# Two expert layers of a decoder on one core: sums copied out by token half, normalization shared between VectorE and ScalarE, last rows stored in two pieces

## What is computed

```python
def _layernorm(x, axis=-1, eps=1e-05):
    m = jnp.mean(x, axis=axis, keepdims=True)
    v = jnp.var(x, axis=axis, keepdims=True)
    return (x - m) / jnp.sqrt(v + eps)

x = _layernorm(x + _L0_attn_ref(x, ...))              # layer A
x = _layernorm(x + _L0_xattn_ref(x, ctx_2048, ...))   # layer B
x = _layernorm(x + _L0_ffn_ref(x, ...))               # layer C: 64 experts of 96 units, top 8
x = _layernorm(x + _L1_attn_ref(x, ...))              # layer D: linear attention
x = _layernorm(x + _L1_xattn_ref(x, ctx_2048, ...))   # layer E
x = _layernorm(x + _L1_ffn_ref(x, ...))               # layer F: 8 experts of 176 units, top 2, and a shared one of 704
```

## Time and profile before

| what | value |
|---|---|
| median of 3 runs | 999.08 us |
| lowest and highest run | 995.08 and 999.41 us |
| the profiled execution's own time | 999.09 us |
| its span, first to last instruction | 997.3 us |
| TensorE busy | 953.6 us, 96% |
| VectorE busy | 635.7 us, 64% |
| ScalarE busy | 443.1 us, 44% |
| mean granted TensorE clock | 0.991 of full |

### The profile page before, as it was taken

The page is one execution under the profiler, slowest core; times in us unless marked ns, Lnnn a source line. Parts: engine busy times, 40 slices in busy tenths (PEclk is TensorE's granted clock), DMA queues, the critical chain, the costliest instruction groups (busy, mean ns, idle before and its releaser), DMA issues. The chain is left out here.

```text
span 997.3 us, 18763 instructions
## 1 busy us (share of the span) xinstructions
PE 953.6 (96%) x6147; PEld 754.6 (76%) x6147; DVE 635.7 (64%) x1474; ACT 443.1 (44%) x862; POOL 311.9 (31%) x514
## 2 busy tenths in 40 slices
PE   6999999999999999999999999988999998999994
PEld 5788887688888888888887855667877775888883
DVE  3676777655655555555556666688778845555555
ACT  4777886432233322222222223326767773333321
POOL 1133123244444444444446303210000015344430
PEclk9999999999999999999999999999999998999997
DMA  8000000256433333333333000011111111655501
GB/s 280 23 17 18 2 2 1 57 156 185 144 133 120 112 113 109 112 111 112 112 111 103 21 0 11 6 36 36 31 37 33 32 66 25 134 145 111 112 19 42
DMA packets 37423, 75.55 MB, mean 76 GB/s; under 512 B 7121, under 2 KB 18365, under 8 KB 37222
## 3 DMA queue, kind: packets, MB, share of 16 engines
q1 hardware_dynamic: 37074, 74.53, 26.3%
q0 software_dynamic: 288, 0.23, 0.2%
HBM read 67.57 MB, written 2.40 MB: 70 GB/s over the span
## 5 line engine op out<-in xcount | busy, mean ns | idle before, releaser
L1059 PE MATMUL ps<-shared 128*128 128x512 f32 x1560 | 380.1, 393 | 0.6 <-POOL shared L2112 0.5
L1059 PEld LDWEIGHTS ps<-shared 128*128 128x128 f32 x1560 | 293.9, 189 | 66.7 <-issue 5.0
L1483 ACT ACTIVATE shared<-pT 128x512 fp32r<-128x512 f32 x130 | 82.2, 632 | 286.5 <-DVE pT L1910 286.5
L2110 POOL CAST shared<-wraw 128x512 fp32r<-128x512 f32 (+1 forms) x130 | 91.3, 703 | 298.0 <-PE ps L1085 275.4
L1913 DVE TENSOR_TENSOR al<-pT,shared 128x512 fp32r<-128x512 f32 x130 | 120.4, 926 | 92.4 <-ACT shared L1483 92.4
L1902 DVE TENSOR_TENSOR e<-e,ps 128x512 f32<-128x512 f32 x130 | 89.4, 688 | 124.4 <-PE ps L1059 120.2
L1085 PE MATMUL ps<-shared 128*128 128x512 f32 x520 | 162.0, 393 | 0.3 <-DVE al L1913 0.2
L2112 POOL TENSOR_TENSOR shared<-wraw,shared 128x512 fp32r<-128x512 f32 (+1 forms) x130 | 133.5, 1027 | 10.4
L1085 PEld LDWEIGHTS ps<-shared 128*128 128x128 f32 x520 | 97.5, 188 | 22.4 <-DVE al L1913 1.2
L1477 ACT ACTIVATE e<-ps 128x512 f32<-128x512 f32 x130 | 77.7, 598 | 77.3 <-PE ps L1059 77.3
L1910 DVE TENSOR_TENSOR pT<-e,kbd 128x512 f32<-128x512 f32 x130 | 100.0, 769 | 7.1
(11 more groups left out here) (228 smaller groups left out, 1376.7 us busy)
## 6 DMA issues: line engine op xcount, KB each, us to landing
kbd<-combine_C SPq DMA_DIRECT2D x46, 512.0 KB
wraw<-in_C_w SPq DMA_DIRECT2D x48, 384.0 KB, 8.2
kbd<-combine_F SPq DMA_DIRECT2D x15, 512.0 KB
wraw<-in_F_w SPq DMA_DIRECT2D x17, 384.0 KB, 7.0
kbd<-kbd SPq DMA_DIRECT2D x96, 32.0 KB, 1.9
kT<-kbd SPq DMA_DIRECT2D x48, 32.0 KB, 1.8
c_ctx_t<-in_ctx_t SPq DMA_DIRECT2D x1, 1024.0 KB, 9.2
out<-c_x_rows SPq DMA_DIRECT2D x2, 512.0 KB, 2.9
```

The source lines that it names most:

```text
L1059: mm = pe.matmul(GU[t][s], w[u][:, (c * 2 + s) * P:(c * 2 + s + 1) * P], xx[:, c, t * HALF:(t + 1) * HALF], start=(i == 0), stop=(i == 5))
L1483: act.activation(ah[t][:, :], a2[t], ACT.Copy).then_inc(S("ah"), 1)
L2110: pool.tensor_copy(wh[u][:, lo:hi], wraw[k][:, lo:hi]).then_inc(S("m_wh"), 1)
```

## The change

Six parts. (1) In both layers ScalarE copies half 0 of `Y` after the last product of half 0 and half 1 after the last product of half 1. (2) VectorE runs `roots(0)` with the statistics of batches 4 and 5 between its three steps, and those of 6 and 7 behind it (`roots_beside_variances`). (3) A new tile `shift8` holds minus the mean times the reciprocal root, one small VectorE instruction for a half (`shifts`), so that ScalarE can normalize with one activation (scale and bias, one value for each partition). (4) In C ScalarE normalizes batches 2 and 3, VectorE the others; a semaphore `rows23` tells of them, and VectorE raises `xn` by 2 for them once they are there. (5) In F ScalarE normalizes batches 0 to 3, and later 6 and 7; VectorE only 4 and 5. (6) The stores of F are three: batches 0 to 3, 4 and 5, 6 and 7, each behind its own semaphore.

```diff
@@ SyncE, after layer F @@
-            for h in range(2):
-                sp.wait_ge(S("xn"), nb("F", 4 * h + 4))
-                sp.dma_start(out[4 * h:4 * h + 4].rearrange("b p d -> p b d"), X[:, 4 * h:4 * h + 4, :])\
+            for rows, n, have in ((0, 4, "rows03"), (4, 2, "rows45"), (6, 2, "rows67")):
+                sp.wait_ge(S(have), n)
+                sp.dma_start(out[rows:rows + n].rearrange("b p d -> p b d"), X[:, rows:rows + n, :])\
                   .then_inc(S("stored"), 16)
@@ TensorE, pe_expert_x_T @@
-                pe.wait_ge(S("xn"), nb("C", b + 1))
+                if b in (2, 3):
+                    pe.wait_ge(S("rows23"), b - 1)
+                else:
+                    pe.wait_ge(S("xn"), nb("C", b + 1))
@@ ScalarE, act_moe @@
-            act.wait_ge(S("m_down"), nm(L, 2, 2 * n))
-
             for h in range(2):
+                act.wait_ge(S("m_down"), nm(L, 2, 2 * n - 1 + h))
                 for c in range(C):
                     act.activation(ysb[c][:, h * HALF:(h + 1) * HALF], Y[:, 2 * c + h, :], ACT.Copy)\
                        .then_inc(S("m_yt"), 1)
+            def normalized(batches, have):
+
+                for b in batches:
+                    act.activation(X[:, b, :], zsb[b // 4][:, (b % 4) * D:(b % 4 + 1) * D], ACT.Identity,
+                                   scale=rstd8[:, b:b + 1], bias=shift8[:, b:b + 1]).then_inc(S(have), 1)
+
+            act.wait_ge(S("shift"), 4 if L == "C" else 8)
             if L == "C":
+                normalized((2, 3), "rows23")
                 act_expert_x(act, 0)
+            else:
+                normalized(range(4), "rows03")
+                act.wait_ge(S("shift"), 12)
+                normalized((6, 7), "rows67")
@@ VectorE, dve_moe @@
+            def shifts(h):
+
+                half = slice(4 * h, 4 * h + 4)
+                dve.wait_ge(S("rstd"), nb(L, 4 * h + 4))
+                dve.scalar_tensor_tensor(shift8[:, half], agg8[:, half, 0], -1.0, rstd8[:, half], ALU.mult, ALU.mult)\
+                   .then_inc(S("shift"), 4)
...
+                dve.wait_ge(S("newton"), n0 + 8)
+                dve.tensor_tensor(t0, p_, p_, ALU.mult).then_inc(S("newton"), 4)
+                statistics(4)
+                dve.wait_ge(S("newton"), n0 + 12)
+                dve.scalar_tensor_tensor(t1, v_, -0.5, t0, ALU.mult, ALU.mult).then_inc(S("newton"), 8)
+                statistics(5)
+                dve.wait_ge(S("newton"), n0 + 20)
+                dve.scalar_tensor_tensor(rstd8[:, 0:4], t1, 1.5, p_, ALU.add, ALU.mult).then_inc(S("rstd"), 4)
+                if L == "C":
+                    shifts(0)
+                    normalized((0, 1), "xn")
+                statistics(6)
+                if L == "F":
+                    shifts(0)
+                statistics(7)
...
             residual(0)
             variances(0)
             residual(1)
-            roots(0)
+            roots_beside_variances()
+            roots(1)
+            dve.wait_ge(S("rstd"), nb(L, B))
             if L == "C":
-                normalized(0)
-            variances(1)
-            if L == "F":
-                normalized(0)
-            roots(1)
-            normalized(1)
+                dve.wait_ge(S("rows23"), 2)
+                dve.sem_inc(S("xn"), 2)
+                normalized(range(4, 8), "xn")
+            else:
+                shifts(1)
+                normalized((4, 5), "rows45")
```

More of the change, by code:

```diff
@@ L142, in build @@
         newton8 = sb("newton8", [P, 5, 8])
+        shift8 = sb("shift8", [P, B])
         stats8 = sb("stats8", [P, B, 6])
@@ L412, in _ @@
             moe_loads(sp, "F")
-            for h in range(2):
-                sp.wait_ge(S("xn"), nb("F", 4 * h + 4))
-                sp.dma_start(out[4 * h:4 * h + 4].rearrange("b p d -> p b d"), X[:, 4 * h:4 * h + 4, :])\
+            for rows, n, have in ((0, 4, "rows03"), (4, 2, "rows45"), (6, 2, "rows67")):
+                sp.wait_ge(S(have), n)
+                sp.dma_start(out[rows:rows + n].rearrange("b p d -> p b d"), X[:, rows:rows + n, :])\
                   .then_inc(S("stored"), 16)
-            sp.wait_ge(S("stored"), 32)
+            sp.wait_ge(S("stored"), 48)
         def pe_T(pe, dst, w, src):
@@ L1959, in roots, with normalized @@
                    .then_inc(S("rstd"), 4)
-            def normalized(h):
-                dve.wait_ge(S("rstd"), nb(L, 4 * h + 4))
-                for b in range(4 * h, 4 * h + 4):
-                    dve.tensor_scalar(X[:, b, :], zsb[h][:, (b % 4) * D:(b % 4 + 1) * D], agg8[:, b, 0:1],
-                                      rstd8[:, b:b + 1], ALU.subtract, ALU.mult).then_inc(S("xn"), 1)
+            def normalized(batches, have):
+                for b in batches:
+                    dve.tensor_scalar(X[:, b, :], zsb[b // 4][:, (b % 4) * D:(b % 4 + 1) * D], agg8[:, b, 0:1],
+                                      rstd8[:, b:b + 1], ALU.subtract, ALU.mult).then_inc(S(have), 1)
@@ new lines, in shifts, with roots_beside_variances, statistics @@
+            def shifts(h):
+                half = slice(4 * h, 4 * h + 4)
+                dve.wait_ge(S("rstd"), nb(L, 4 * h + 4))
+                dve.scalar_tensor_tensor(shift8[:, half], agg8[:, half, 0], -1.0, rstd8[:, half], ALU.mult, ALU.mult)\
+                   .then_inc(S("shift"), 4)
+            def roots_beside_variances():
+                v_, p_, t0, t1 = (newton8[:, n, 0:4] for n in range(4))
+                n0 = nb(L, 0) * 5
+                def statistics(b):
+                    dve.wait_ge(S("z"), nb(L, b // 2 * 2 + 3))
+                    dve.bn_stats(stats8[:, b, :], zsb[1][:, (b % 4) * D:(b % 4 + 1) * D]).then_inc(S("stats"), 1)
+                dve.wait_ge(S("newton"), n0 + 8)
[13 more added lines that the diff above has]
+                statistics(7)
+                for b in range(4, 8):
+                    dve.wait_ge(S("stats"), nb(L, b + 1))
+                    dve.bn_aggr(agg8[:, b, :], stats8[:, b, :]).then_inc(S("agg"), 1)
+                dve.wait_ge(S("agg"), nb(L, 8))
+                dve.tensor_scalar(newton8[:, 0, 4:8], agg8[:, 4:8, 1], EPS, None, ALU.add).then_inc(S("newton"), 4)
```

## The result

| | before | changed |
|---|---|---|
| median of 21 runs, us | 999.01 | 1001.32 |
| lowest and highest | 995.08, 1000.61 | 997.98, 1003.62 |
| the profiled execution's own time | 999.09 | 1001.99 |
| its span | 997.3 | 1000.0 |

The ratio is 1.0023, with a 95% interval of 1.0014 to 1.0032: slower by 2.3 us, where 2.35 faster was forecast. It is within the 0.5% called no change, but outside the range, and on the other side.

What follows compares the result with a forecast made beforehand. Matmuls were taken to bound the expert layers' long loops, one engine-to-engine chain the ends of C and F. F's 2.15 plus C's 0.2 gave 2.35 us off 999.09: 996.7 us, range 992.5 to 999.3.

Steps and rivals of the forecast that it cites:

- the two slower ones: Rival 3 (clock falls in C, 1000.1 us, chance 0.06) and rival 4 (stores, 999.4 us, chance 0.02).
- rival 1: Early layer F: the clock's fall is missing in most changed runs, saving 3.4 to 4.0 us more; 992.7 to 993.3; chance 0.21.
- The end of F: Layer F from 979 us on: one chain between engines, forecast 2.15 us shorter in all.
- Copies by halves: End of F: half 0 copied beside half 1's products, so transposes start earlier; 1.13 us gained, bounds 0.9 and 1.16.
- Root steps beside statistics: End of F, first root step to second epsilon: statistics fill waits between small steps; 0.42 us gained, bounds 0 and 0.5.
- GpSimd's stretch: End of F, behind the second epsilon: GpSimd's wait of 1.18 us was to stay.
- The last rows: End of F behind the third root step: normalizations shared with ScalarE, store split; 0.6 us gained, bounds -0.2 and 0.85.
- rival 4: F's stores: the second piece's fixed time comes behind the first piece; sum +0.3 us, 999.4; chance 0.02.
- The end of C: Layer C, about 581 to 596 us: batch 3 ready earlier for transposes; 0.2 us gained, bounds -0.3 and 0.6.
- Rival 2: The chain's gains are mostly taken back, only 1.13 us stays; about 998.0 us; chance 0.12.
- Rival 3: End of C: TensorE's idle stretch grows to some 0.75 us, the clock falls, 3.4 us lost; 1000.1; chance 0.06.
- the low run of 995.08: Lowest of three earlier runs, 4.0 us under the next, read as one without the clock's fall in early layer F.

Runs made afterwards that it cites:

- experiment 7: Changed kernel with `shift8` allocated last and only `al` moved by 64 bytes, to a multiple of 128; median 993.30 us, ratio 0.9951 to the kernel before.
- experiment 12: As experiment 7, but batches 4 to 7 stored in one piece once all four are there; 992.56 us, one run.
- experiment 11: As experiment 7, but in layer C the statistics of batches 4 and 5 stand behind the first two normalizations; median 993.69 us, ratio 0.9960.
- experiment 9: Changed kernel with `shift8` last, `al` moved by 32 bytes, and TensorE reading `ah` in place of `al`; 991.29 us, one run.
- 3: Changed kernel with `shift8` 64 bytes wide instead of 32 in its old place, moving all tiles behind it; median 993.79 us, ratio 0.9956.
- 8: Changed kernel with `shift8` last, `wraw` moved by 64 bytes and `al` by 256; median 997.12 us, ratio 0.9984.
- experiment 15: As experiment 11, but `al` at a multiple of 256 and TensorE's other operands moved too, most to multiples of 256; median 989.82 us, ratio 0.9929.
- experiments 1: Kernel before with only an unused tile of 32 bytes a partition added where the change put `shift8`; median 1000.01 us, ratio 1.0035.
- 5: Changed kernel with `shift8` last and only `al` moved by 32 bytes; median 1000.16 us, ratio 1.0016.
- 10: Changed kernel with `shift8` last, `al` moved by 64 bytes, and TensorE reading `ah` in place of `al`; 990.11 us, one run.

## Why the prediction was wrong

**The step that failed** is the first one: "So the long loops of the expert layers are bound by matmuls, and this change does not touch them." The added tile, part 3 of the change, was costed at its instruction alone. It moved `al` by 32 bytes, and 130 half blocks grew by 0.033 us each, 4.3 us, against 2.3 gained: 2.0 slower from these two alone, where the runs give 2.3 (1.4 to 3.2). The sentence even names what to fear: where TensorE sets the pace, whatever lengthens one of its matmuls is paid at every turn. No rival had it; the two slower ones stayed away, and rival 1 did not come either: the changed kernel's trace has its 3.4 us of lower clock, and its lowest run, 997.98, is above the forecast.

**The end of F, by its own steps.** Copies by halves: from the last product to the first root step 6.40 before (981.41 to 987.81), 5.00 now: 1.40 gained, forecast 1.13; not only is the wait gone but also the gap behind the last product, since transposes follow products in one stream. Root steps beside statistics: 987.81 to 990.21 was 2.40, 991.40 to 993.48 is 2.08: 0.32, forecast 0.42. The four pairs of a small step and a statistics took 1.61, to 993.01, forecast 1.56, and the aggregations with the hand-off 0.47, forecast 0.4. GpSimd's stretch, forecast at nothing, gave 0.12. The last rows: from the third root step to the span's end 4.97 before, 4.52 now: 0.45, forecast 0.6; the shift came at T + 0.30 instead of 0.20. Sum 2.29, forecast 2.15. The activation of a batch took 0.60 and one each 0.49 (four in 2.08), forecast 0.57 and 0.46. Two pieces in flight overlap: in experiment 7 the second piece left at 987.90 and took 2.2 us, and the third left 0.47 behind it, at 988.37, and took 2.5. With the 0.46 us of experiment 12 that ends rival 4. The Trainium skill, "DMA: Bandwidth & Descriptors", on the anatomy of one DMA, gives its fixed cost for DMAs issued from GpSimd, and these are SyncE's; the 2.6 and 3.2 us estimated from it compare with 2.2 to 2.5 and 2.9 to 3.0 measured, and it did not speak against this split.

**The end of C**: 0.2 forecast, 0.00 measured. The statistics between the root steps were sized nearly rightly: from the first root step to the third pass 0.82 us, before 0.54, so 0.28 more where 0.24 was forecast. The copies gave more than the 0.29 forecast: the transposes start 0.87 behind the filler instead of 1.33, and the first root step 6.03 instead of 6.55. So the third root step comes 6.85 behind the filler (590.88) and came 7.09 behind it before, 0.24 earlier. But the shift starts only 0.25 behind it, VectorE then stands idle for 0.24 us between shift and first normalization, and the first row is ready at 7.91 behind the filler instead of 7.70. I had let batch 3 set the end of the transposes; it is the first row that does, since TensorE needs 1.20 for the eight, and they ended 9.16 behind the filler, as before (9.17). Why the 0.24 stand there is open: experiment 11, without the statistics, does not have them, and they and the 0.28 are nearly all of its 0.54.

**Rival 2** (gains taken back on the chain) has no support at F's end. **Rival 3**: TensorE was idle for 1.3 us, 590.70 to 591.99, more than the 0.75 reckoned, and no fall of the clock followed.

**The clock.** TensorE's windows in the changed kernel, which answer to the earlier trace rows:

```profile
820.00:830.00 10.00, 8.48 (x85) 1.00 0.06 22
830.00:840.00 10.00, 8.30 (x43) 1.00 0.14 42
840.00:850.00 10.00, 10.00 (x24) 0.66 0.08 11
```

Again 3.4 us lost (10 x 0.34), now between 840 and 850 alone. Of 17 traces, 16 have a fall near the start of F, worth 1.7 us (0.83 in one window) or twice that; only experiment 12 has none there, and 3.4 us at 180 us instead:

```profile
180.00:190.00 10.00, 9.69 (x29) 0.66 0.04 9
...
830.00:840.00 10.00, 9.20 (x41) 1.00 0.00 1
840.00:850.00 10.00, 10.00 (x41) 1.00 0.50 85
```

Four traces have a second fall of 1.7 us, at 180 (experiment 9), 670 (3 and 7) or 690 us (8). The 21 runs of the kernel before spread over 5.5 us without two separate groups. So the low run of 995.08 need not be one without the fall, as I read it; falls of either size at more than one place are enough. That the clock's monitor is not reset by a kernel's start, as the Trainium skill has it ("TensorE: Matmul & The Clock Gate"), agrees with sizes and places that change from run to run; but 16 of 17 traces have one near the start of F, so where it falls is not chance alone.

## What to carry to other kernels

A new tile is an edit of every tile allocated behind it. Before costing a change's instructions, list which tiles move, and where TensorE sets the pace in a loop put what it streams at multiples of 256 bytes, or allocate new small tiles last. Measure it: it paid for `al`, while the other operands of experiment 15 showed no gain. When a loop that nobody edited changes its step by less than 1%, compare addresses before instructions: an unused tile in the old kernel settles it in one run.

## What the runs showed of the hardware that was not expected

A matmul of 512 fp32r columns takes longer if the tile it streams begins off a multiple of 256 bytes: by about 7 ns at 128 past one, 17 at 64 past, 33 at 96 past, of some 227 ns for one (4.080 / 18). The values are means over a loop, the same whether all tiles moved (the changed kernel, experiments 1 and 3) or `al` alone (5 and 7), and they come with what TensorE reads and not with what VectorE writes (9 and 10). Nothing was tried at other remainders, with other types or with the stationary operand.
